# Half of the attention's values computed inside the attention loop, and weight quantizing shared by two preparation stages

## The reference

```python
mod = (silu(c) @ wmod).reshape(B, 6, 1, 256)          # sa, ca, ga, sb, cb, gb
h = layernorm(x) * (1 + ca) + sa
q, k = h @ query_proj, h @ key_proj                   # 16 heads of 16
v = h @ value_proj                                    # 16 heads of 64
attn = softmax(q k / 4, axis=queries)
x = x + ga * (attn @ v) @ output_proj
h = layernorm(x) * (1 + cb) + sb
x = x + gb * ffn(h)       # down(silu(gate(h)) * up(h)), hidden size 704
# every operand of gate, up and down is quantized to FP4 in blocks of 16 first
```

## Time and profile before

| | before |
|---|---|
| time, median of 3 runs | 1696.1 us (1695.29 to 1697.58) |
| profiled execution, its own time | 1700.96 us |
| profiled execution, span | 1699.6 us |
| TensorE busy | 1646.5 us (97%), 15446 matmuls |
| VectorE busy | 1591.2 us (94%) |
| ScalarE busy | 1364.8 us (80%) |
| GpSimd busy | 779.4 us (46%) |

### The profile page before, as it was taken

One profiled execution on the slowest core, in us unless ns is written; L12 is line 12 of the kernel. 1 busy time (PEld: TensorE's weight loads), 2 busy tenths in 40 slices (PEclk: granted clock), 3 DMA queues, 4 the chain that ended last, 5 costly groups with the idle time before them and its releaser, 6 DMA issues.

```text
span 1699.6 us, 38849 instructions
## 1 busy us (share of the span) xinstructions
PE 1646.5 (97%) x15446; PEld 818.5 (48%) x15446; DVE 1591.2 (94%) x1726; ACT 1364.8 (80%) x2490; POOL 779.4 (46%) x1625
## 2 busy tenths in 40 slices
PE   9999999999999999999999999999999999999998
PEld 8743333333332333664333333333333379999997
DVE  6989999999999999769999999999999869988887
ACT  5389999999999999638999999999999933333332
POOL 3024444544444445303544454566645447644552
PEclk8999999999999999999999999999999999999999
DMA  6202111111111112411111112111111544434420
GB/s 223 72 2 70 51 51 49 45 45 56 61 51 51 47 45 75 156 48 35 46 52 47 45 45 67 53 51 51 46 45 45 154 133 125 149 125 148 153 67 19
DMA packets 83103, 123.15 MB, mean 72 GB/s; under 512 B 4706, under 2 KB 69098, under 8 KB 82922
## 3 DMA queue, kind: packets, MB, share of 16 engines
q1 hardware_dynamic: 82506, 120.15, 22.3%
q10 hardware_dynamic: 416, 0.53, 0.1%
HBM read 74.52 MB, written 46.15 MB: 71 GB/s over the span
## 4 chain that ended last, share of the span: by engine, by line
DVE 65%; PE 29%; ACT 2%; issue 2%; POOL 1%; DMA 1%; SPq 0%; ACTq 0%; POOLq 0%; DVEq 0%
DVE nm L1070 60%; PE acc L436 11%; PE slot L436 9%; PE acc L603 5%; ACT e_sb L812 2%; PE slot L659 1%; DVE ost L1083 1%; PE slot L574 1%; DVE v_sb L1030 1%; DMA v_sb<-in_wmod 0%; PE acc L634 0%; PE slot L457 0%; DVE qs L1137 0%; DMA qk_parts<-e_sb 0%; DVE e_sb L1125 0%
## 5 line engine op out<-in xcount | busy, mean ns | idle before, releaser
L1070 DVE TENSOR_REDUCE nm<-slot 128x1 f32<-128x1024 f32 x1024 | 1166.1, 1213 | 8.1 <-PE slot L574 5.9
L812 ACT ACTIVATE e_sb<-slot,nm 128x1024 f32<-128x1024 f32 x1024 | 1137.3, 1113 | 23.9 <-DVE nm L1070 19.0
L603 PE MATMUL acc<-e_sb,vp 64*64 64x512 f32 x8192 | 1060.7, 594 | 6.7 <-DVE ost L1083 4.7
L574 PE MATMUL slot<-stq,stk 64*64 64x512 f16 x4096 | 412.0, 388 | 21.6 <-ACT e_sb L812 21.6
L574 PEld LDWEIGHTS slot<-stq,stk 64*64 64x64 f16 x4096 | 117.7, 103 | 626.7 <-ACT e_sb L812 589.5
L603 PEld LDWEIGHTS acc<-e_sb,vp 64*64 64x64 f32 x8192 | 283.4, 132 | 188.4 <-issue 74.2
L1305 POOL TENSOR_TENSOR dlt<-nm 128x4 f32<-128x4 f32 x128 | 25.9, 202 | 422.7 <-DVE nm L1070 422.7
L812 ACT ACTIVATION_READ_ACCUMULATOR e_sb<-slot,nm 128x1 f32 x1024 | 199.6, 195 | 0.0
L1296 POOL TENSOR_TENSOR vp<-v_sb,fac 128x512 f32<-128x512 f32 x128 | 133.6, 1044 | 10.2 <-POOL fac L1286 0.3
L1282 POOL TENSOR_TENSOR rtot<-tot,mone 128x4 f32<-128x4 f32 x128 | 132.8, 1038 | 10.0
L1276 POOL TENSOR_TENSOR wsum<-cor,ssum 128x8 f32<-128x8 f32 x128 | 26.0, 203 | 233.4 <-ACT cor L840 233.4
(11 more groups left out here) (180 smaller groups left out, 1940.3 us busy)
## 6 DMA issues: line engine op xcount, KB each, us to landing
o_r<-o_heads SPq DMA_DIRECT2D x32, 1024.0 KB, 7.4
stk<-qk_parts SPq DMA_DIRECT2D x128, 128.0 KB
o_heads<-ost_hi SPq DMA_DIRECT2D x64, 256.0 KB, 3.4
o_heads<-ost SPq DMA_DIRECT2D x64, 256.0 KB, 4.1
v_sb<-in_x SPq DMA_DIRECT2D x16, 512.0 KB, 6.6
qk_parts<-e_sb SPq DMA_DIRECT2D x32, 256.0 KB, 2.9
stq<-qk_parts SPq DMA_DIRECT2D x128, 64.0 KB
out<-e_sb SPq DMA_DIRECT2D x32, 128.0 KB, 1.8
```

The costliest lines, as they stand in the source:

```text
L574: mm = pe.matmul(slot[s][side * VD:(side + 1) * VD, c * 512:(c + 1) * 512], stk[c * 64:c * 64 + 64, h % 2, i * P + side * VD:i * P + (side ...
L603: mm = pe.matmul(acc[half * VD:(half + 1) * VD, c * 512:(c + 1) * 512], vp[rows, g % 3, gi, half, :], e_v[rows, j % ERING, n0:n0 + 512], s ...
L812: act.activation(e_v[:, j % ERING, half * 1024:(half + 1) * 1024], slot[u % 3][:, :], ACT.Exp, bias=nm[:, g % 4, i, half:half + 1], accum_ ...
L1070: dve.tensor_reduce(nm[:, g % 4, i, half:half + 1], slot[u % 3][:, :], AX.X, ALU.max, negate=True).then_inc(maxed.sem)
```

## The change

Values of heads 0 to 7 are made as before, but one use per tile. Values of heads 8 to 15 are made in the attention: tile t in turn j = 7 + 8t, behind that turn's two scores, in the score slot whose turn it is (a turn of its own in the rotation of three), and ACT copies them out. The turned tokens now lie in the places of `v_sb` that these values take later, instead of in `e_sb`, where the exponentials go; the weights to quantize move to `e_sb`. Gate and up are quantized in two parts: tiles 0 to 4 in the first preparation (9 steps of 1280 elements), tiles 5 to 10 in the second (9 steps of 1536), before down (18 steps of 704, with one small product more in each last step). In `down` the last chunk holds its 64 rows of data twice, and against the second copy stands the low part of the weights: two matmuls instead of three. Loads of x are issued as eight transfers instead of four, and the last head of the first sequence is stored after the first four stores of the second preparation instead of before its weight loads.

```diff
+def late_tile(j):
+    t, rest = divmod(j - AFTER, EVERY)          # AFTER, EVERY = 7, 8
+    return t if rest == 0 and 0 <= t < NT else None
+def score_turns():
+    turns = []
+    for j in range(JT):
+        turns += [(j, 0), (j, 1)]
+        if late_tile(j) is not None:
+            turns.append((j, 2))
+    return turns, {what: t for t, what in enumerate(turns)}
...
+        by_dve = range(EARLY + 1, NT, 2)
+        by_act = [i for i in range(NT) if i not in by_dve]
+        def slot_read(b, t):
+            j, half = turns[t]
+            return late_v.past(b * NT + late_tile(j)) if half == 2 else exped.past(b * UNITS + 2 * j + half)
+        def slot_of(j, half):
+            return slot[turn_of[j, half] % 3]
...
+        def late_values(b, j):
+            pe.wait_ge(*slot_read(b, turn_of[j, 2] - 3))
+            value_products(slot_of(j, 2)[:, 0:512], late_tile(j), 1).then_inc(late_mm.sem)
...
         def scores(b, j, half):
-            s = u % 3
+            t = turn_of[j, half]
+            s = t % 3
-            if u >= 3:
-                pe.wait_ge(*exped.past(b * UNITS + u - 3))
+            if t >= 3:
+                pe.wait_ge(*slot_read(b, t - 3))
...
                         if jv >= 0 and not begins:
                             attend(b, 2 * jv + half)
+                    if late_tile(j) is not None:
+                        late_values(b, j)
                     if begins:
                         attend(b, 2 * jv)
                         attend(b, 2 * jv + 1)
                     if j < NT - EARLY:
-                        for c in range(2):
-                            values(b, EARLY + j, c)
+                        values(b, EARLY + j)
...
+        def take_late_values(b, j):
+            t = late_tile(j)
+            act.wait_ge(*late_mm.past(b * NT + t))
+            act.copy(v_t[:, t, 512:HV], slot_of(j, 2)[:, 0:512]).then_inc(late_v.sem)
...
             for i in range(EARLY):
-                for c in range(2):
-                    values(b, i, c)
+                values(b, i)
                 if b == 0 and i == 3:
                     mod_rows_pe()
+            turn_gate_up(b)
             if b:
                 turn_down()
-            else:
-                turn_gate_up()
...
-                    if b == 0 and g == NG - 1:
+                    if g == NG - 1 or b and g and r % 2:
                         weight_step(b, step)
                         step += 1
...
-            for i in range(EARLY):
-                take_values_dve(b, i)
-                if b == 0 and i == 3:
-                    mod_rows_dve()
-                for s in range(step, min(step + 2, 18)):
-                    weight_step(b, s)
-                step += 2
+            for s in range(step, 27 if b else 9):
+                weight_step(b, s)
+            if b == 0:
+                mod_rows_dve()
...
-            products(down_at(i), [(hqT_lo[:, i % 2, c, :], hqT_hi[i % 2][:, c // 2, c % 2 * P:(c % 2 + 1) * P], wdb_lo[b][:, c, :],
-                                            wdb_hi[b][:, c, :]) for c in range(FCH)]).then_inc(down_mm.sem)
+            last = FCH - 1
+            products(down_at(i), [(low_part[c], high_part[c], wdb_lo[b][:, c, :], wdb_hi[b][:, c, :]) for c in range(last)],
+                     [(high_part[last], wdb_hi[b][:, last, :]), (low_part[last], wdb_hi[b][:, last, :])])
```

More of the change, by code:

```diff
@@ L33 @@
 EARLY = 9
+AFTER, EVERY = 7, 8
 FCH = 6
@@ L177, in wide, with turned @@
             return ap.unsqueeze(2).to_broadcast([P, nb, 16])
[L180 to L185, removed]
-        tmp = region(v_sb, 10240, 2, D)
[L187 to L191, removed]
+        GU = ((0, 5), (5, 11))
+        wgu_r = [region(e_sb, 12288, 5, D), region(e_sb, 4096, 6, D)]
+        wd_r = [region(e_sb, 12288, FCH * P), region(e_sb, 12288 + FCH * P, FCH * P)]
+        w_xn = place("w_xn", [P, 1536], OST_AT)
+        w_big = vp[:, :, :, :, :].rearrange("p a b c d -> p (a b c d)")
+        wm = region(e_sb, 4096, 2, 1536)
+        mrow = region(e_sb, 14336, 4, D)
+        tmp = region(v_sb, 10240, 2, D)
+        v_t = v_sb[:, :].rearrange("p (t n) -> p t n", n=HV)
+        v_r = place("v_r", [P, NT, HV], V_AT, F32R)
+        x_v = v_t[:, 0:8, 0:512].rearrange("p a (b d) -> p a b d", d=D)
+        def turned(full, part, k, tiles):
+            at = 512 + part * 256 + k * P
+            return full[:, tiles, at:at + P]
         wq_lo = place("wq_lo", [P, 2, 256], WQ_AT, F32R)
@@ L382, in sync_program @@
                             part_r[g % 2][:, r]).then_inc(part_out[g % 2][r].sem, 16)
+                    if b and g == 0:
+                        store_head(b - 1, H - 1)
                 for p in range(2):
@@ L429, in sync_program, with products @@
                 sp.wait_ge(*out_out[s].past((TILES - 1 - s) // 3))
-        def products(o, pairs):
+        def products(o, pairs, others=()):
             for n, (xl, xh, wl, wh) in enumerate(pairs):
                 for m, (a, w) in enumerate(((xh, wh), (xh, wl), (xl, wh))):
-                    mm = pe.matmul(o, a, w, start=(n == 0 and m == 0), stop=(n == len(pairs) - 1 and m == 2))
+                    mm = pe.matmul(o, a, w, start=(n == 0 and m == 0),
+                                   stop=(n == len(pairs) - 1 and m == 2 and not others))
+            for n, (a, w) in enumerate(others):
+                mm = pe.matmul(o, a, w, start=False, stop=(n == len(others) - 1))
             return mm
@@ L508, in mod_rows_pe, with turn_gate_up @@
                 mm.then_inc(rows_mm.sem)
[L510 to L516, removed]
+        def turn_gate_up(b):
+            pe.wait_ge(*gu_quant.past(b))
+            others = GU[b][1] - GU[b][0] - 4
+            for n in range(3):
+                o = take_quarter(b, "gu", 3 * b + n)
+                these = [(i, n) for i in range(4)] if n < 2 else [(4 + i, k) for k in range(2) for i in range(others)]
+                for m, (i, k) in enumerate(these):
+                    mm = pe.transpose(o[:, m * P:(m + 1) * P], wgu_r[b][:, i, k * P:(k + 1) * P], ident[:, :])
                 mm.then_inc(gu_turn.sem)
@@ L840, in attend_act @@
                         act.activation(cor[:, g % 4], dlt[:, g % 4], ACT.Exp).then_inc(cor_made.sem)
-                if j < NT - EARLY:
+                if j < NT - EARLY and EARLY + j in by_act:
                     take_values_act(b, EARLY + j)
+                if late_tile(j) is not None:
+                    take_late_values(b, j)
                 if j == JT + 2 and b == B - 1:
@@ L1069, in maximum @@
             dve.wait_ge(*scored.past(b * UNITS + u))
-            dve.tensor_reduce(nm[:, g % 4, i, half:half + 1], slot[u % 3][:, :], AX.X, ALU.max, negate=True).then_inc(maxed.sem)
+            dve.tensor_reduce(nm[:, g % 4, i, half:half + 1], slot_of(j, half)[:, :], AX.X, ALU.max, negate=True).then_inc(maxed.sem)
         def attend_dve(b):
```

189 lines of the change are left out of this document (99 added, 90 removed).

## The result

The changed kernel takes 1733.29 us (median of 4 runs, 1731.59 to 1734.32) against 1696.84 us before in the same session (1695.29 to 1698.56): a ratio of 1.0211, 95% interval 1.0198 to 1.0223, 36.4 us more. Forecast were 28.5 more and 1724 us, range 1704 to 1738.

A forecast was written before the change was run, and what follows sets the result against it. VectorE's maxima bound the attention, with TensorE only 0.40 us ahead. Late values +58.8, clock +1.5, first preparation -9.5, first turns -7.3 and -7.8, second preparation -3.4, `down` -3.8: +28.5 on 1696.1, 1724 us, range 1704 to 1738.

The forecast's parts named there:

- late value inside a head: Attention, j % 16 = 15: VectorE stands still for 1.2 us per late value, bounds 0.9 and 1.6.
- late value where a head begins: Attention, j % 16 = 7 from 23: late value ahead of both `attend` calls costs 2.6 us, bounds 1.2 and 3.0.
- first maximum, first preparation: First preparation: the first stack comes last, maxima start at 69.0 instead of 78.49, -9.5 us, bounds -15.4 to about 0.
- clock behind the idle TensorE: First preparation: after about 6 us idle, TensorE runs the first value and scores at half speed, +1.5 us (0 to 3).
- first turns, first sequence: First seven attention turns, one value use per tile instead of two: -7.3 us (-5 to -9).
- first turns, second sequence: The same first seven turns in the second sequence: -7.8 us (-5 to -9).
- second preparation: Second preparation: stack loads begin 2.4 us later, maxima start at 747.4 instead of 750.79, -3.4 us (-7 to +2).
- `down`: Feed-forward: one matmul of 18 less in each of 32 tiles, -3.8 us (-4 to 0).
- late values find room: Rival on attention: PE's position in the ring does not matter, only its work; 1674 us, chance 0.08.
- the stack isn't last: Rival on both preparations: maxima from 63.2 and 744, no fall of the clock; 1713 us, chance 0.12.
- a head's beginning costs no more: Rival on attention: a late value where a head begins costs no more than another, 20 us less; 1704 us, chance 0.09.
- the stack lands near 78: Rival on the first preparation: the first stack lands near 78, 9.5 us later; 1734 us, chance 0.08.

The follow-up runs named there:

- experiment 3: The changed kernel without late values, ScalarE copying the values of heads 0 to 7 in their place: 1673.59 us, 0.9858 of the kernel before.
- experiment 4: The changed kernel with each stack loaded in sixteen transfers of outermost dimension 16 instead of eight with 2: 1720.86 us, 1.0138 of the kernel before.
- experiment 6: The kernel before with two matmuls for the last chunk of `down`, GpSimd's small product behind its main one: 1694.4 us, 0.9982.
- experiment 1: The changed kernel with late values at j % 16 = 3 and 11 instead of 7 and 15: 1718.67 us, 1.0123 of the kernel before.
- experiment 5: The kernel before with two matmuls for the last chunk of `down`, GpSimd's small product ahead of its main one: 1696.4 us, 0.9994.
- experiment 8: The kernel before with two-matmul last chunk of `down`, small product behind the main one, and stacks in sixteen transfers: 1695.16 us, 0.9981.
- experiment 2: The changed kernel with the late value issued behind both `attend` calls where a head begins: 1719.22 us, 1.0128 of the kernel before.
- experiment 10: The changed kernel with one matmul instead of six per late value, at j % 16 = 3 and 11: 1698.39 us, 1.0002 of the kernel before.
- experiment 11: The changed kernel with three matmuls instead of six per late value, inside heads: 1694.95 us, 0.9987 of the kernel before.
- experiment 9: The changed kernel with one matmul instead of six per late value, at the old places: 1718.25 and 1732.78 us in two runs, 1.0165.

## Why the prediction was right

The forecast was +28.5 us. The profiled executions differ by 1732.7 - 1699.6 = 33.1, the medians by 36.4. By its own steps:

| step | forecast | profile |
|---|---|---|
| late value inside a head | 1.2 | 1.18 |
| late value where a head begins | 2.6 | 2.67 |
| all late values, both sequences | +58.8 | +59.9 (experiment 3) |
| first maximum, first preparation | -9.5 | -10.9 |
| clock behind the idle TensorE | +1.5 | +3.3 (experiment 4) |
| first turns, first sequence | -7.3 | -7.8 |
| first turns, second sequence | -7.8 | -7.0 |
| second preparation | -3.4 | -2.9 |
| `down` | -3.8 | -1.3 |

First maximum: 67.59 against 78.49. The stack landed 66.8 - 47.93 = 18.9 us after its first issue, for which halving the total had given 18.35; SP began it 2.1 us earlier than in the earlier trace rows, which was not counted. First turns: 82.41 - 61.15 = 21.26 in experiment 4, which has no fall of the clock, against the 29.0 of the earlier trace rows; 784.87 - 762.32 = 22.55 against 29.51. Second preparation: the first maximum is 11.5 us later than in the earlier trace rows, with 14.45 brought along. `down`: the chains are 34.4 us apart at the second sequence's last head boundary (1368.54 against 1334.13) and 33.1 at the end.

**Where the sizes were off.** `down` gave 1.3 instead of 3.8. Its matmul was worth 4.2 (experiment 6); GpSimd's small product took 1.6 back, which the bounds named as possible, and 1.3 went to a fall of TensorE's clock in the last tile, which the forecast did not have. The same feed-forward takes 362.87 us behind the last head boundary in experiment 1 and 364.16 in the changed kernel; windows of the last tile, changed kernel, then experiment 1:

```profile
1726.00:1728.00 2.00, 2.00 (x11) 2.00 (x11) 0.74 (x1) 0.00 (x0) 0.00 (x0) 0.50 0.00 0
```

```profile
1710.00:1712.00 2.00, 2.00 (x18) 1.93 (x18) 1.38 (x2) 0.00 (x0) 0.00 (x0) 1.00 0.00 0
```

The clock's term of the first preparation was half of what it is, 1.8 short, for its second fall was not foreseen. That the first sequence still came out within 0.4 us is luck in part: the first maximum was 1.4 earlier and the first turns 0.5 shorter than forecast. The steps of the second sequence came out 1.8 us dearer in sum. So 2.5 + 0.4 + 1.8 make the 4.6 between 28.5 and 33.1, but for rounding.

The other 3.4 is no step that the forecast names. The profiled execution of before took 1700.96 us with a mean granted clock of 0.994; other executions of it, in the experiments' sessions, had 0.995 to 0.999 and 1699.9 to 1695.3 us, by and large the lower the clock the longer. The forecast put the difference of one profile on a median, and that profile was a long one. Part of its surplus can be placed: in experiments 5, 6 and 8, whose first preparation has the same work but for one small fill by GpSimd, the first maximum comes at 76.94, 76.23 and 76.97 instead of 78.49. Against these the changed kernel gains 8.6 to 9.4 us there and not 10.9. The rest of the surplus was not placed.

**The rivals.** That late values find room (1674): out by 60 us. That the stack isn't last (1713): the row with 5.97 us of waiting for `stk` decides against it. That a head's beginning costs no more (1704): experiments 1 and 2 show 0.9 to 1.2 us more for each of 14. That the stack lands near 78: it landed at 66.8. VectorE's idle time was forecast at 60 us and is 85.7: 60.5 of it is the late values' (experiment 3), and 10.44 + 6.59 = 17.0 stand ahead of the first maxima of the two sequences (4.8 before), which the forecast left out.

**What is new beside the forecast.** Its price for a late value was right for six matmuls, and it holds for work of that size alone. Experiments 10 and 11 show a floor of 0.72 us that leaving out matmuls did not remove.

## What to carry to other kernels

Work that is moved into a loop paced by one engine costs the pacing engine whatever exceeds the lead of the engine that does the work, here 0.40 us by the forecast's reading, even though that engine is idle elsewhere; and a visitor in a rotation of three buffers has a price of its own, one buffer less for one round. Put an instruction that waits behind those that need not: the order of two calls was worth 13 us here. After a bound is taken away, look at once for what comes last instead, here a load on two of sixteen DMA engines: more engines brought 12 us after the change, and nothing before it. And one profile is one execution: compare it with the median before a forecast is put on it.

## What the runs showed of the hardware

- TensorE's granted clock fell to 0.50 behind an idle stretch of 5.97 us. It also fell at places where the same instructions and waits did not always bring it down: in experiment 9 at seven heads' beginnings of the second sequence and at none of the first, with waits of 0.72 and 1.17 us and one short matmul between, 1.6 us a head; once in experiment 4 at such a beginning (a head of 42.13 us instead of 40.86); and in the last tile, in the changed kernel and not in experiment 1, 1.3 us.
- Stack loads on sixteen engines ran at 62 to 98 GB/s, with SP issuing 32 or 64 KB every 0.6 us, on two at 45 to 53.
- The mean granted clock of executions of the kernel before varied from 0.994 to 0.999, and their times from 1700.96 to 1695.3 us.
